# Sparse attention stage: the division of the turned products moved from VectorE to ScalarE and GpSimd

## The reference

```python
scores = jnp.einsum('bhqa,bhka->bhqk', q, k) * SCALE
top_vals = jax.lax.top_k(scores, TOP_K)[0]
cutoff = top_vals[..., -1:]
masked = jnp.where(scores >= cutoff, scores, -jnp.inf)
w = jax.nn.softmax(masked, axis=-1)
e = jnp.einsum('bhqk,bhka->bhqa', w, v)
...
x = x + jnp.tanh(g_xattn[3]) * _L3_xattn_ref(_layernorm(x, axis=-1), ctx_1024, ctx_1024, L3_xattn_Wq, L3_xattn_Wk)
```

## Time and profile before

| | |
|---|---|
| median of 3 runs | 3078.91 us |
| lowest, highest | 3070.96, 3082.48 us |
| the profiled execution's own time | 3081.14 us |
| its span | 3079.3 us |
| busy: TensorE, VectorE, ScalarE, GpSimd | 90%, 66%, 60%, 46% of the span |
| granted TensorE clock, mean | 0.935 |
| first and last division of the stage | 1887.5 and 2644.2 us from the span's start |

### The profile page before, as it was taken

How to read it: one execution, slowest core, us unless ns; L and a number is a source line. 1 busy time by engine, 2 the same in 40 slices (tenths; PEclk the granted TensorE clock), 3 DMA queues, 4 the chain that set the end, 5 groups by cost and what they waited for, 6 DMA issues and landing times. The chain is left out here.

```text
span 3079.3 us, 70583 instructions
## 1 busy us (share of the span) xinstructions
PE 2774.2 (90%) x21912; PEld 2136.3 (69%) x21912; DVE 2031.7 (66%) x7995; ACT 1840.5 (60%) x5346; POOL 1428.6 (46%) x1748
## 2 busy tenths in 40 slices
PE   7999969986998989999999999988899984597999
PEld 5888854433766668888888777666677762386776
DVE  5445536664653456666666459999999999686433
ACT  5777734443543346666666468888888874453333
POOL 2122117762442434444444238787878786452000
PEclk9999979997998999999999899999999995697999
DMA  3000024323763311111111000000000000001000
GB/s 115 6 5 6 5 52 88 82 60 113 263 220 126 120 56 55 54 54 54 54 54 54 23 10 14 14 13 13 13 13 13 13 14 33 3 18 36 8 10 10
DMA packets 99461, 151.83 MB, mean 49 GB/s; under 512 B 11312, under 2 KB 39488, under 8 KB 98752
## 3 DMA queue, kind: packets, MB, share of 16 engines
q1 hardware_dynamic: 99296, 149.96, 16.5%
HBM read 103.33 MB, written 46.47 MB: 49 GB/s over the span
## 5 line engine op out<-in xcount | busy, mean ns | idle before, releaser
L1899 POOL TENSOR_TENSOR l2a_probs<-l2a_probs,l2a_inv 128x1024 f32<-128x1024 f32 x128 | 242.3, 1893 | 369.4 <-DVE l2a_inv L2065 369.2
L2010 ACT ACTIVATE l2a_probs<-l2a_s_ps,l2a_nm 128x256 f32<-128x256 f32 x512 | 236.6, 473 | 199.2 <-DVE l2a_nm L2041 199.2
L2847 DVE MAX8 l3a_top<-l3a_work 128x8 f32<-128x128 f32 x1536 | 314.2, 276 | 0.0
L2424 POOL TENSOR_SCALAR l3a_above<-l3a_score,l3a_top 128x128 f32<-128x128 f32 x504 | 294.1, 601 | 16.6 <-DVE l3a_top L2847 8.5
L2565 PE MATMUL l3a_l2o_ps<-net_arena 128*128 128x128 f32 x1952 | 256.1, 295 | 33.8 <-ACT net_l1f_gate L2681 33.4
L2565 PEld LDWEIGHTS l3a_l2o_ps<-net_arena 128*128 128x128 f32 x1952 | 249.6, 210 | 45.5 <-ACT net_l1f_gate L2681 37.0
L2849 DVE MATCH_REPLACE8 l3a_work<-l3a_top,l3a_work 128x128 f32<-128x128 f32 x1024 | 268.9, 275 | 0.0
L2552 PE MATMUL l3a_l2h_ps<-net_cols,net_arena 128*128 (+1 forms) x1024 | 251.9, 388 | 14.7 <-ACT net_arena L2716 12.8
L2552 PEld LDWEIGHTS l3a_l2h_ps<-net_cols,net_arena 128*128 128x128 f32 x1024 | 184.8, 191 | 67.2 <-ACT net_arena L2716 25.3
L721 ACT ACTIVATE l0a_probs<-l0a_score_ps,l0a_nm 128x128 f32<-128x128 f32 x512 | 180.1, 383 | 73.5 <-DVE l0a_nm L770 73.5
L2716 ACT ACTIVATE net_arena<-l3a_l2h_ps,net_l2f_b 128x256 f32<-128x256 f32 x496 | 203.6, 492 | 12.4 <-PE l3a_l2h_ps L2552 11.0
(11 more groups left out here) (532 smaller groups left out, 7152.6 us busy)
## 6 DMA issues: line engine op xcount, KB each, us to landing
kv_ahead<-l1a_kept SPq DMA_DIRECT2D x128, 256.0 KB, 2.7
l0f_code<-code_rows SPq DMA_DIRECT2D x32, 512.0 KB, 11.2
l2a_kT<-kv_ahead SPq DMA_DIRECT2D x64, 256.0 KB, 2.6
l2a_v<-kv_ahead SPq DMA_DIRECT2D x64, 256.0 KB, 2.6
l1a_shift<-neg_top SPq DMA_DIRECT2D x16, 512.0 KB, 4.9
l1f_chosen<-mask_code SPq DMA_DIRECT2D x64, 128.0 KB, 3.1
keys_ahead<-l1f_keys_kept SPq DMA_DIRECT2D x32, 256.0 KB, 3.2
l3a_kT<-keys_ahead SPq DMA_DIRECT2D x32, 256.0 KB, 2.7
```

The lines of the kernel that those rows point to most:

```text
L1899: pool.tensor_tensor(p[:, :, :], p[:, :, :], per_row(inv[c % 2][a][:, :, :].rearrange("p i o -> p (i o)"), KV), ALU.mult).then_inc(scaled, 1)
L2010: act.activation(probs[c % 2][a][:, 2 * i + odd, :], s_ps[a][odd][:, i * KV:(i + 1) * KV], ACT.Exp, bias=nm[c % 2][a][:, i, odd:odd + 1], ...
L2424: ins = pool.tensor_scalar(above[:, i, :], score[c % 4][:, h, :], top[c % 2][:, ROUNDS - 1, h, 7:8], None, ALU.is_ge)
L2847: ins = dve.max(t[:, step // 2, h, :], src)
```

## The change

VectorE's `divide` is gone. In its place:

- ScalarE has a new step `take_out`, first in its list, for tile t-3: it waits for `o_turned` and copies all nine columns of each head out of PSUM into a new tile `o_raw` of 128x144, which signals `o_ready`.
- GpSimd's `add_attention`, at its old place at the end of the list, first raises the ninth column to the power -1 (128x16, the exponent from a tile `neg_one` that is filled at the start), waits for it, multiplies by it (128x128), waits again, and adds.
- The semaphore `o_ready`, for which `apply` waits before it writes the bank again, now comes from ScalarE's copy. A new one, `o_read`, keeps that copy from overwriting `o_raw` early.
- In the draining lists `take_out` comes first on ScalarE, and VectorE has only `negate_last` and `mask_last`; GpSimd's `add_attention` stays ahead of `negate_max`, as it was.

```diff
+        inv, neg_one = s.sb("inv", [P, H]), s.sb("neg_one", [P, H])
+        o_raw = s.sb("o_raw", [P, H, DA + 1])
...
-                pool.wait_ge(filled, 4)
+                pool.memset(neg_one[:, :], -1.0).then_inc(filled, 1)
+                pool.wait_ge(filled, 5)
...
                 def add_attention(q, c):
                     wait(pool, o_ready, q, 1, c + 1)
+                    pool.tensor_tensor(inv[:, :], o_raw[:, :, DA:DA + 1].rearrange("p h o -> p (h o)"), neg_one[:, :], ALU.pow
+                                       ).then_inc(inv_ready, 1)
+                    wait(pool, inv_ready, q, 1, c + 1)
+                    wait(pool, x_done, q, 1, c)
+                    pool.tensor_tensor(o_norm[:, :, :], o_raw[:, :, 0:DA], per_row(inv[:, :], DA), ALU.mult
+                                       ).then_inc(o_read, 1)
+                    wait(pool, o_read, q, 1, c + 1)
...
+                def take_out(q, c):
+                    wait(act, o_turned, q, 1, c + 1)
+                    wait(act, o_read, q, 1, c)
+                    act.activation(o_raw[:, :, :], o_ps[:, :, 0:DA + 1], ACT.Copy).then_inc(o_ready, 1)
...
-                schedule(act, [(for_part(exps, 0), 1), (for_part(exps, 1), 1), (for_part(take_y, 0), 1 - AHEAD),
+                schedule(act, [(take_out, 3), (for_part(exps, 0), 1), (for_part(exps, 1), 1), (for_part(take_y, 0), 1 - AHEAD),
...
-                         draining=[(for_part(take_p, 0), 2), (for_part(exps, 0), 1), (for_part(exps, 1), 1), (for_part(take_p, 1), 2),
+                         draining=[(take_out, 3), (for_part(take_p, 0), 2), (for_part(exps, 0), 1), (for_part(exps, 1), 1), (for_part(take_p, 1), 2),
...
-                        if (half, step) == (1, 2) and c == NB - 1:
-                            divide(q, c - 2)
-
-                def divide(q, c):
-                    wait(dve, o_turned, q, 1, c + 1)
-                    wait(dve, x_done, q, 1, c)
-                    dve.reciprocal(inv[:, :], o_ps[:, :, DA:DA + 1].rearrange("p h o -> p (h o)")).then_inc(inv_ready, 1)
-                    wait(dve, inv_ready, q, 1, c + 1)
-                    dve.tensor_tensor(o_norm[:, :, :], o_ps[:, :, 0:DA], per_row(inv[:, :], DA), ALU.mult
-                                      ).then_inc(o_ready, 1)
...
-                def divide_last(q, c):
-                    if c >= NB - 2:
-                        divide(q, c)
...
-                schedule(dve, [(divide, 3), (for_part(cutoffs, 0), 0), (for_part(cutoffs, 1), 0),
+                schedule(dve, [(for_part(cutoffs, 0), 0), (for_part(cutoffs, 1), 0),
                                (in_group(measure, 1), 1 - AHEAD)], loops=0,
-                         draining=[(divide_last, 3), (negate_last, 1), (mask_last, 2)])
+                         draining=[(negate_last, 1), (mask_last, 1)])
```

More of the change, by code:

```diff
@@ L2270, in l3_attention @@
         pT = [s.sb(f"pT{i}", [P, Q4, P]) for i in two]
-        inv = s.sb("inv", [P, H])
+        inv, neg_one = s.sb("inv", [P, H]), s.sb("neg_one", [P, H])
+        o_raw = s.sb("o_raw", [P, H, DA + 1])
         o_norm = s.sb("o_norm", [P, H, DA])
@@ L2306, in l3_attention @@
         o_ps = ov_ps[:, :].rearrange("p (h d) -> p h d", h=H)
-        v_blank, o_taken, o_turned = s.sem("v_blank"), s.sem("o_taken"), s.sem("o_turned")
+        v_blank, o_taken, o_turned, o_read = s.sem("v_blank"), s.sem("o_taken"), s.sem("o_turned"), s.sem("o_read")
         k_loaded, v_loaded = ([s.sem(f"{n}_loaded{i}") for i in two] for n in "kv")
@@ L2875, in negate_last @@
                                       None, ALU.mult).then_inc(nm_ready, 1)
-                def divide_last(q, c):
-                    if c >= NB - 2:
-                        divide(q, c)
                 def mask_last(q, c):
-                    if c < NB - 1:
-                        return
                     dve.wait_ge(masked, NQ * c + NQ // 2)
```

## The result

The changed kernel takes 3091.15 us (median of 6 runs, 3088.01 to 3095.36); the kernel before 3078.8 (6 runs, 3070.96 to 3082.48). The ratio is 1.0042, 95% interval 1.0028 to 1.0057: 12.35 us slower, clear of no change. The ratio lies just under 0.5%, and its interval reaches from 0.28% to 0.57%, so on which side of 0.5% the change falls isn't settled. The forecast was 3093 us, 14.3 us more. The profiled execution took 3092.75 us, its span is 3091.0 us.

The account below looks back on a forecast made before the run. VectorE was taken to bound the kernel before and GpSimd after the change; 6.6 + 4.4 + 3.3 = +14.3 us on the median 3078.9 gave 3093 us, range 3074 to 3106.

Parts of the forecast that it names:

- Who binds: Steady steps: GpSimd's pair of tiles becomes 52.2 us against VectorE's 50.2, so GpSimd binds instead of VectorE.
- threshold of 2.5 us a tile: Steady steps: break-even addition to GpSimd; a power of 1.9 us or less would leave VectorE the bound.
- The power: GpSimd's exponent -1 on 128x16: 2.91 us, from rows with exponent -0.5; bounds 0.20 and 3.28 us.
- the cheap rival: GpSimd's power costs only 0.2 us, VectorE stays the bound: 3065 us; chance 0.12.
- to tile 31: Steady steps up to VectorE's start of tile 31: 2609.9 us in the trace against 2603.3 before, +6.6 us.
- to the negation: End of the stage, GpSimd up to tile 31's negation: 23.4 us against 19.0 before, +4.4 us.
- the last division: Very end of the stage: 4.0 us with nothing beside it against 0.66 before, +3.3 us.
- VectorE's lead: Steady steps: VectorE runs ahead until tile c's search meets tile c-2's mask, then waits there once a pair.
- Cheap division: GpSimd's addition is only 0.9 us a tile and stays hidden: 3065 us; chance 0.12.
- Costlier division: GpSimd's power takes 3.28 us or its product 0.6; at 4.0 us a tile 3106 us; chance 0.18.
- ScalarE in the loop: ScalarE's steps spill over and delay the masks by 0.4 to 0.8 us a pair: 3098 to 3104 us; chance 0.07.
- The port: GpSimd's added work slows VectorE's searches through a shared port: some 3110 us; chance 0.03.

Follow-up runs that it names:

- e1: Changed kernel with GpSimd's power replaced by a product of the same operands, division left out: 3063.61 us, ratio 0.9953 to the kernel before.
- e2: Changed kernel with the power taken of 8 of the 16 heads only, the others' division left out: 3070.81 us, ratio 0.9963 to the kernel before.
- e7: Changed kernel with the scaling of the values moved from GpSimd to the end of ScalarE's step: 3076.81 us, ratio 1.0002 to the kernel before.
- e3: Changed kernel with a second, unused power of the same size ahead of the first: 3181.84 us, ratio 1.0325 to the kernel before.
- e4: Changed kernel with the reciprocal back on VectorE, and tile 31's negation and mask ahead of tile 29's division: 3062.15 us, ratio 0.9954.

## Why the prediction was right

**Who binds.** Right. GpSimd's pair came out at 52.08 us against 52.2; VectorE's, seen alone in e1 and e2, at 50.17 against 50.2. The threshold of 2.5 us a tile is borne out from both sides: 2.2 us cost nothing in the steady part (e2); 2.9 us, which is what GpSimd has net in e7 (3.5 less the 0.6 of the values), did cost, with pairs of 50.90 us, and so did 3.5; and beyond the threshold nearly all is paid (e3: 5.83 of the 5.98 us that two powers of 2.91 with their gaps make).

**The power.** The step on which everything stood: taken from powers with another exponent, at 2.91 us; it is 2.935 in the median. Its row and the product's (ns lowest, median, highest):

```profile
L2436 POOL TENSOR_TENSOR l3a_inv<-l3a_o_raw,l3a_neg_one x32: 2912/2935/2944, 1908.9 to 2653.8; 128x16 f32<-128x16 f32 x32
L2440 POOL TENSOR_TENSOR l3a_o_norm<-l3a_o_raw,l3a_inv x32: 406/407/412, 1911.9 to 2656.8; 128x128 f32<-128x128 f32 x32
```

So the power with -1 has no short way here, and the cheap rival falls. The product, put between half and the whole of a 128x256 row, was 0.407 us for 0.42. The power takes about twelve times VectorE's 0.24 us for the same reciprocals. The Trainium skill's factor of 1.96 (GPSIMD Engine Reference, section 3.1) does not carry over to it: by an estimate with that factor the change would have been a gain.

**The sum.** Its three terms: to tile 31 +6.6 expected, +7.5 measured; to the negation +4.4, +4.3; the last division +3.3, +3.4. Together 14.3 and 15.2 in the stage. The median moved by 12.35 us. The difference between 15.2 and 11.6 in the two profiled executions is that the one after reached the stage 2.7 us sooner; what follows the stage, 0.7 us shorter, made up the rest. The forecast's 14.3 lies between the median's 12.35 and the stage's 15.2.

**What was wrong in it.** The sum said that VectorE's lead ends at the mask of the tile before the last, once a pair. It never waited there. It waits at the row statistics, for the experts' last add of the same step, 1.8 us a pair, as here in VectorE's order of time:

```profile
2505.67 0.49 DVE L2872 BATCH_NORM_STATS2 l3a_stats<-net_x 128x6 f32<-128x128 f32 x2 [1.81 <-POOL net_x L2461]
```

I had read `measure`'s wait for `x_added` in the code and not followed it: that add is the last of four and ends in a short step some 3.3 us behind the mask. So VectorE's lead is shorter, which moves no pair's length but starts the last tiles' searches elsewhere than I worked out.

That the first term came out so close is in part luck. GpSimd's negations at step 28, before and after:

```profile
2526.77 0.24 POOL L2408 TENSOR_SCALAR l3a_nm<-l3a_top 128x8 f32<-128x8 f32 x1 [0.69 <-DVE l3a_top L2847]
...
2538.11 0.46 POOL L2410 TENSOR_SCALAR l3a_nm<-l3a_top 128x8 f32<-128x8 f32 x2
```

Counted from the second negation of step 3 in each trace, GpSimd is 14.3 us late there (the second of the two joined ones starts some 0.2 us into its row), where I had 16. But of this lateness only 6.8 us were made good until tile 31, and not 9.4: VectorE's last wait is again at the row statistics, at 2557.73, and from there two whole searches lead to tile 31's at 2608. Misses of 1.7 and 2.6 us all but cancelled.

ScalarE's copy takes 0.29 us, not 0.4, and it does wait for GpSimd, 46.3 us in all, where I had said that its waits are met early. `exps` behind it would have waited for the same queue: before, the exponentials waited 30.0 us for `negate_max` in the same 640 us, and now 4.0. So it costs nothing (in e1 it is there too, and the pairs are VectorE's).

**The rivals.** Cheap division: out, but e1 shows what it would have given, 3063.6 us for the 3065 of the rival. Costlier division: out by the rows. ScalarE in the loop: out, since no mask waited for an exponential from 1900 to 2540 us, and in e7, where ScalarE does more, they waited 1.7 us in all. The port: MAX8 is at 0.275 us in the median with GpSimd nearly full, as before, and the pace of the search is the same too, 12.45 us from one half's first MAX8 to the next's in both kernels.

## What to carry to other kernels

An engine under the busiest one is not free: what it can take is its idle time per turn less what the busiest engine gets shorter, here 2.5 us a tile, and past that nearly every us is paid. When work moves to another engine, price the very operation there: the product takes 0.41 us on GpSimd for VectorE's 0.29, the power twelve times the reciprocal. Split it at that line: the reciprocal stayed on VectorE for 0.1 us and the product moved, which gave 0.46% (with the better order at the end, some 1 us of it by the estimate above), where moving both lost 0.42%.

## What the runs showed of the hardware

- GpSimd's power takes nearly the same time with exponent -1 as with -0.5: 1.67 us for 8 elements per row and 2.94 for 16, against 1.64 and 2.91, about 0.16 us for each element more.
- VectorE's reciprocal of 128x16 between two searches, with nobody on VectorE who waits for it, cost 0.10 us a tile though its row is 0.27 us long; reciprocal, wait and product had cost 0.48.
- An instruction's length on GpSimd hardly changed when the engine went from 83% to 93% busy (the mask's comparison 0.601 and 0.604 us in the median, the add 0.454 and 0.456), and VectorE's search kept its pace of 12.45 us a half.
- The length of a short instruction's row is not its cost in the queue: in e4 the MAX8 on `l3a_work` have rows of 0.308 us in the median against 0.275 in the changed kernel, and yet the half of a search up to the reciprocal takes 12.44 us, as there.
